# Half of a rotary product moved from GpSimd to VectorE in a fused attention and expert block

## The reference

```python
q, k, v = split_heads(x @ Wq.T + bq), split_heads(x @ Wk.T + bk), split_heads(x @ Wv.T + bv)
q = q * cos + _rotate_half(q) * sin
k = k * cos + _rotate_half(k) * sin
attn = softmax((q @ k.T) * scale)
x = _layernorm(x + (attn @ v) @ Wo.T + bo)
x = _layernorm(x + ffn(x))
```

## Time and profile before

| what | us |
|---|---|
| three runs: lowest, median, highest | 222.32, 223.0, 223.11 |
| the profiled execution, device time | 222.24 |
| its span in the trace | 220.4 |
| busy: VectorE | 180.7 |
| busy: TensorE | 173.0 |
| busy: ScalarE | 169.4 |
| busy: GpSimd | 141.3 |

### The profile page before, as it was taken

How to read it: one execution, slowest core, us unless ns; L and a number is a source line. 1 busy time by engine, 2 the same in 40 slices (tenths; PEclk the granted TensorE clock), 3 DMA queues, 4 the chain that set the end, 5 groups by cost and what they waited for, 6 DMA issues and landing times.

```text
span 220.4 us, 5283 instructions
## 1 busy us (share of the span) xinstructions
PE 173.0 (79%) x1839; PEld 122.4 (56%) x1839; DVE 180.7 (82%) x522; ACT 169.4 (77%) x357; POOL 141.3 (64%) x123
## 2 busy tenths in 40 slices
PE   1879678686767886887788679758697998999991
PEld 0223345464645664666567456636484675777781
DVE  6989969958796987898789969797989788486483
ACT  3878786777589978976997899688567989649624
POOL 6070777398989799798979997899850033021514
PEclk9999999889999999999999999999999999999999
DMA  6233423131214322121313121212120000001012
GB/s 234 88 82 85 103 70 83 31 82 36 63 37 122 105 67 62 36 62 38 86 32 77 41 63 40 61 47 53 48 51 1 4 3 3 0 3 48 0 52 95
DMA packets 13002, 12.63 MB, mean 57 GB/s; under 512 B 3152, under 2 KB 11952, under 8 KB 12976
## 3 DMA queue, kind: packets, MB, share of 16 engines
q1 hardware_dynamic: 12832, 12.03, 20.5%
q10 hardware_dynamic: 144, 0.26, 0.3%
HBM read 2.73 MB, written 1.05 MB: 17 GB/s over the span
## 4 chain that ended last, share of the span: by engine, by line
PE 27%; DVE 26%; POOL 18%; ACT 7%; issue 7%; DMA 3%; POOLq 0%; DVEq 0%; ACTq 0%
DVE row_max L1212 10%; POOL by_sin L1042 9%; POOL by_cos L1042 8%; DVE roped L1171 8%; PE ps_o L600 5%; PE ps_s L565 5%; DMA qk<-mT_sb 3%; PE ps_t L455 3%; PE ps_m L507 3%; DVE o_sb L1235 3%; PE ps_s L403 2%; ACT raw L830 2%; ACT probs L865 2%; ACT x L877 2%; PE ps_o L476 2%
## 5 line engine op out<-in xcount | busy, mean ns | idle before, releaser
L865 ACT ACTIVATE probs<-ps_t 128x512 bf16<-128x512 f32 x128 | 76.7, 616 | 27.8 <-PE ps_t L455 27.5
L1212 DVE TENSOR_REDUCE row_max<-ps_s 128x2 bf16<-128x512 f32 x120 | 80.3, 674 | 4.8 <-PE ps_s L403 3.0
L1042 POOL TENSOR_TENSOR by_cos<-raw,in_b 128x1024 bf16<-128x1024 bf16 x25 | 53.0, 2122 | 22.1 <-DVE roped L1171 19.8
L830 ACT ACTIVATE raw<-ps_m,bqk 128x256 bf16<-128x256 f32 x128 | 53.6, 489 | 6.0 <-PE ps_m L388 5.9
L403 PE MATMUL ps_s<-qk 128*128 128x256 bf16 x218 | 41.7, 278 | 18.6 <-DVE row_max L1212 16.1
L1042 POOL TENSOR_TENSOR by_sin<-raw,in_b 128x1024 bf16<-128x1024 bf16 x25 | 53.0, 2122 | 0.0
L455 PE MATMUL ps_t<-qk 128*128 128x256 bf16 x256 | 49.3, 276 | 1.8 <-DMA qk<-mT_sb 1.7
L476 PE MATMUL ps_o<-v_sb,probs 128*128 128x65 bf16 x512 | 36.2, 195 | 1.0 <-DVE row_max L1212 0.6
L476 PEld LDWEIGHTS ps_o<-v_sb,probs 128*128 128x128 bf16 x512 | 31.7, 98 | 6.8 <-issue 1.7
L388 PE MATMUL ps_m<-in_b 128*128 128x256 bf16 x128 | 27.1, 304 | 9.4 <-DMA in_b<-in_packed_b 4.3
L403 PEld LDWEIGHTS ps_s<-qk 128*128 128x128 bf16 x218 | 14.6, 98 | 25.4 <-issue 10.9
(11 more groups left out here) (136 smaller groups left out, 250.5 us busy)
## 6 DMA issues: line engine op xcount, KB each, us to landing
qk<-roped SPq DMA_DIRECT2D x128, 64.0 KB, 2.0
in_b<-in_packed_b SPq DMA_DIRECT2D x1, 768.0 KB, 5.8
out<-y_sb SPq DMA_DIRECT2D x3, 256.0 KB, 2.2
in_f<-in_packed_f SPq DMA_DIRECT2D x1, 586.0 KB, 4.0
in_b<-in_packed_b SPq DMA_DIRECT2D x1, 512.0 KB, 4.4
in_b<-in_packed_b ACTq DMA_DIRECT2D x1, 256.0 KB, 3.7
qk<-mT_sb SPq DMA_DIRECT2D x16, 4.0 KB, 1.7
bv_rep<-in_repeated_bv SPq DMA_DIRECT2D x1, 256.0 KB, 2.9
```

The lines of the kernel that those rows point to most:

```text
L830: last = nc.scalar.activation(raw[:, u % 2, g, a, half, :], ps_m[bank][:, half * S:half * S + S], ACT.Identity, bias=bqk[:, a, chunk:chunk ...
L865: nc.scalar.activation(probs[:, h % 4].rearrange("p c s -> p (c s)"), ps_t[h % 2][:], ACT.Exp, scale=DH ** -0.5).then_inc(exp_done, 1)
L1042: last = nc.gpsimd.tensor_tensor(by[:, g].rearrange("p a h s -> p (a h) s"), raw[:, u % 2, g].rearrange("p a h s -> p (a h) s"), table[:]. ...
L1212: nc.vector.tensor_reduce(row_max[:, u % 2, h % 4, h // 4, :], of_head[:].rearrange("p (t s) -> p t s", s=S), AX_X, ALU.max, negate=True). ...
```

## The change

For units 5 to 15, GpSimd's fourth product (by_sin of group 1) covers only q (a = 0). The k part (a = 1), 128x512 elements, is made by VectorE in the new function `half_product`, in the slot of the unit's sums and directly ahead of them, behind the layer norm's variance in odd slots. It counts up `own_ready`, on which the sums wait, as does ScalarE before it overwrites `raw` two units later. The condition `T > 1` stands for units 5 and later.

```diff
@@ -823,8 +823,8 @@
                     act.wait_ge(rope_ready, 2 * (u - 2) + 2)
                 if g == 0 and a == 0 and u >= 5:
                     act.wait_ge(products_ready, u - 4)
-                if g == 0 and a == 0 and u == 6:
-                    act.wait_ge(own_ready, 2)
+                if g == 0 and a == 0 and u >= 6:
+                    act.wait_ge(own_ready, u - 4)
                 for half in range(2):
                     chunk = 4 * (u % 2) + 2 * g + half
                     last = nc.scalar.activation(raw[:, u % 2, g, a, half, :], ps_m[bank][:, half * S:half * S + S],
@@ -1039,9 +1039,10 @@
                     pool.wait_ge(rope_ready, 2 * u)
                 if piece % 2 == 0:
                     pool.wait_ge(raw_ready, 4 * u + piece + 2)
-                last = nc.gpsimd.tensor_tensor(by[:, g].rearrange("p a h s -> p (a h) s"),
-                                               raw[:, u % 2, g].rearrange("p a h s -> p (a h) s"),
-                                               table[:].unsqueeze(1).broadcast_to([P, 4, S]), ALU.mult)
+                of = slice(0, 1 if u > 4 and piece == 3 else 2)
+                last = nc.gpsimd.tensor_tensor(by[:, g, of].rearrange("p a h s -> p (a h) s"),
+                                               raw[:, u % 2, g, of].rearrange("p a h s -> p (a h) s"),
+                                               table[:].unsqueeze(1).broadcast_to([P, 2 * of.stop, S]), ALU.mult)
                 if piece == pieces(u) - 1:
                     last.then_inc(products_ready, 1)
 
@@ -1196,13 +1197,20 @@
                         dve.wait_ge(sin_ready, 3)
                     else:
                         dve.wait_ge(products_ready, u - 2)
-                    if u == 4:
-                        dve.wait_ge(own_ready, 2)
+                    if u >= 4:
+                        dve.wait_ge(own_ready, u - 2)
                     if u >= 2:
                         dve.wait_ge(qk_in[(u - 2) % 4], copies_in(u - 2))
                     rotate(u, both, 0).then_inc(rope_ready, 1)
                 if k == 3:
                     rotate(u, both, 1).then_inc(rope_ready, 1)
+
+            def half_product(u):
+
+                dve.wait_ge(rope_ready, 2 * u)
+                dve.wait_ge(raw_ready, 4 * u + 4)
+                nc.vector.tensor_tensor(by_sin[:, 1, 1], raw[:, u % 2, 1, 1], sin_sb[:].unsqueeze(1).broadcast_to([P, 2, S]),
+                                        ALU.mult).then_inc(own_ready, 1)
 
             def row_maxima(u, h, it):
                 dve.wait_ge(s_ready, n(it, UH, u, h + 1))
@@ -1360,6 +1368,8 @@
                 if s["out"] and T != 15:
                     ln_one((T - 3) // 2, 2)
                     ln_one((T - 3) // 2, 3)
+                if s["rotate"] and T > 1:
+                    half_product(T + 3)
                 if s["rotate"] and T != 1:
                     rope(T + 3, 2)
                     rope(T + 3, 3)
```

## The result

| | before | after |
|---|---|---|
| median of 11 runs, us | 222.66 | 224.07 |
| lowest and highest | 222.32, 223.38 | 223.51, 225.27 |
| ratio, 95% interval | | 1.0053 (1.003 to 1.0077) |
| profiled execution, span | 222.24, 220.4 | 224.95, 223.2 |
| VectorE, GpSimd busy | 180.7, 141.3 | 185.7, 130.1 |

A forecast was written before the change was run, and what follows sets the result against it. No engine is full; the order of hand-overs among TensorE, VectorE and GpSimd sets the time. +0.88 (four slot pairs), +0.03 (slots 11 and 12) and -0.57 (slot 2) give +0.34, rounded to +0.3 on 223.0: 223.3 us, range 222.2 to 224.6.

The forecast's parts named there:

- within 0.5%: Whole kernel: time within about 0.5%, 1.1 us, of the kernel before, which a measurement cannot tell from no change; chance 0.72.
- Odd slots charge, even slots give: Slots 3 to 12: VectorE late in odd slots, +0.50 us each; GpSimd late in even ones, 0.28 us gained each.
- The cost of one product on VectorE: Ahead of the sums: a 128x512 bfloat16 product of 0.42 us plus a gap, 0.46 to 0.53, taken as 0.50 us.
- GpSimd's half: GpSimd's fourth product, halved to 128x512, takes 1.06 to 1.16 us and ends 0.96 to 1.06 us earlier, taken as 1.0.
- Slot 2: VectorE's product and GpSimd's half exclude each other, so the sums come 0.57 us earlier instead of 1.0.
- No DMA is added or moved: Transfers: none added or moved; SyncE's copies of the sums start with the sums, 0.50 us later in odd slots.
- the transfer of the row maxima follows the sums at a fixed distance: Behind the sums: the transfer keeps its distance, as the maxima stand behind the sums on VectorE; no cost of its own.
- the priced part: The forecast's slot terms: slot 2's gain, odd slots' charges, even slots' and slot 12's gains; +0.34 us in sum.
- Rival A: Odd slots: GpSimd's power gets between the new product and the sums; +1.2 us, 224.5 us; chance 0.13.
- Rival B: Odd slots: the 0.50 us is absorbed, so only the even slots count; -2.2 us, 220.8 us; chance 0.12.
- Rival C: Slot 2: VectorE and GpSimd do not exclude each other, giving 1.0 us; sum -0.1, 222.9 us; chance 0.12.
- Rival D: GpSimd's fourth product stays at its full 2.12 us despite halved elements; about +5.5 us, 228.5 us; chance 0.03.

The follow-up runs named there:

- The two kernels with one kind of slot: The changed kernel with VectorE's half product in even slots only, 220.44 us, 0.9904; or in odd slots only, 226.27 us, 1.0161.
- the second execution of the change: Profiled execution of the changed kernel itself, run once more on another chip; ratio 1.0056 to the kernel before.
- The pair of kernels that differ in the place of the extra products: Changed kernel with forty added TensorE products, in even slots 2 to 10, 0.999, or in the pauses behind the odd sums, 0.9936.
- the extra products: Eight added 128x128 TensorE products in each odd slot's pause, 3 to 11: on the changed kernel 0.9936, on the kernel before 0.9951.

## Why the prediction was right or wrong

The measured 224.07 us lies in the stated range, 222.2 to 224.6, and 0.8 us above the forecast. Part of that nearness is luck: the forecast of 223.3 was counted from three runs with a median of 223.0, and the kernel before then measured 222.66. Of the change itself +0.3 us was forecast, and 1.2 (by the ratio) to 1.4 us (by the medians) measured. Of the three cases it had called "within 0.5%" the likeliest; the ratio is 1.0053, just beyond that bound, with an interval that reaches to both sides of it. Its own sign of being wrong, two slots together that change by more than 0.5 us, showed twice in the profiled execution: +1.28 us for slots 6 to 8 and +0.66 for 8 to 10. The mechanism it described was right and not complete.

- **Odd slots charge, even slots give.** Right: +0.51 and -0.27 against +0.50 and -0.28, slot 12 at 9.78 us. The two kernels with one kind of slot show both signs by themselves.
- **The cost of one product on VectorE.** Right: 0.42 us and 0.09 to the sums, 0.51 where 0.50 was taken.
- **GpSimd's half.** 1.15 us, the float32 row's 1.16 and not half of 2.12; it mattered only in slot 2, since elsewhere VectorE is the late one.
- **Slot 2.** The sign of the exclusion was right and its size wrong: the gain was 0.78 us, not 0.57. The sum had charged a whole product (0.42 or 0.50); the two instructions met at GpSimd's boundary, and what GpSimd gave, 2.12 - 1.15 = 0.97, lost only the 0.19 us by which its half was lengthened.
- **"No DMA is added or moved", "the transfer of the row maxima follows the sums at a fixed distance".** Right for the issue of the row, 4.23 us behind the sums in slot 6 before and after, and not for its landing: 3.0 us in slot 6, where before it had taken 2.4, and 2.3 in the second execution of the change. The kernel before pays for late rows as well, 1.1 us in slots 6 and 10, so they explain the 2.8 us between the two profiled executions in part, and not the cost of the change. The forecast had seen that one stretch took 10.51 instead of 9.88 us and not asked why.
- **TensorE's clock.** This step was missing. The forecast had "+0.50 each, and everything up to the next sums shifts by as much", and followed the delay along TensorE without asking what a longer pause does to TensorE itself. Three falls behind the longer pauses cost 0.88 us in the one profiled execution of the changed kernel and 0.90 in the other; with the +0.24 us of the priced part that is 1.1 us, near the 1.2 of the ratio. The pair of kernels that differ in the place of the extra products gives 1.2 us with a wide interval. With the extra products in both, the changed kernel and the one before lie at 0.9936 and 0.9951, and their intervals, 0.003 on either side, do not tell 0 from +0.3 us: the priced part is known from the stretches alone.
- **Rival A** did not come: the power began beside the product and the sums kept 1.29 us. **Rival B** did not: even-to-odd stretches are 10.39. **Rival C** did not: slot 2's product and GpSimd's half were both lengthened, though the gain, 0.78 us, lay midway between the forecast's 0.57 and the rival's 1.0. **Rival D** did not: 1.15 us.

## What to carry to other kernels

When work moves from one engine to another in a loop whose slots differ, ask in each kind of slot which of the two is the late one: here the same edit gave 0.27 us where GpSimd was late and cost 0.51 where VectorE was, and doing it in the first kind alone gave 1%. Then look at the longest pause that the delay makes on TensorE and check the granted clock behind it, in several executions, before counting the delay itself as the whole price. And where a repeated stretch has two lengths, find out why before calling either one the normal.

## What the runs showed of the hardware that was not expected

- In slots 3 to 11 a pause of TensorE of 1.37 us was followed by a fall of the clock from 2.4 to 1.2 GHz in 2 cases of 30, one of 1.89 us in 19 of 25; in the first slots pauses of 1.99 to 2.21 us were in 6 of 11. A fall behind an odd pause cost 0 to 0.52 us of the chain, depending on what else was late: nothing where the next sums waited for GpSimd.
- A 4 KB transfer between two places of SBUF landed after 1.7 us, and after 2.3 to 3.0 us in all 31 cases in which a 0.02 MB packet of instructions came 0 to 1.0 us behind its issue. A packet that came 1.5 us or more behind it (14 cases) left the 1.7 us as they were.
- A VectorE product of 128x512 with two SBUF inputs that was called up during a GpSimd product ended 0.27 to 0.30 us behind that product's end, whenever it had been called up (0.53, 1.04, 1.10 us instead of 0.42), and lengthened GpSimd's next by 0.19 us if that began at once. One of 128x256 ended 0.14 to 0.15 us behind it.
